# Layer 0 of a four-layer model: attention scores by single heads in two row tiles, and low parts, cosines and unpacking rearranged

## What is computed

```python
q, k, v = (proj(wq), proj(wk), proj(wv))          # 32 heads of 16
q = _apply_rope(q, sin, cos)                       # x*cos + rot*sin
k = _apply_rope(k, sin, cos)
scores = jnp.einsum('bnth,bnsh->bnts', q, k) * (1.0 / math.sqrt(h))
scores = jnp.where(causal, scores, -jnp.inf)
attn = jax.nn.softmax(scores, axis=-1)
out = jnp.einsum('bnts,bnsh->bnth', attn, v)       # then @ wo.T

Wg, Wu, Wd = _dequant(gate...), _dequant(up...), _dequant(down...)   # (w4 - (z4 + 1)) * s
h = jax.nn.silu(xf @ Wg) * (xf @ Wu)
out = h @ Wd
```

## Time and profile before

| | us |
|---|---|
| median of 3 runs | 2555.86 (2555.06 to 2556.41) |
| the profiled execution | 2561.34 |
| its span | 2559.6 |
| busy: PE / PE weight loads | 2455.2 (96%) / 1962.8 (77%) |
| busy: DVE / ACT / POOL | 1618.1 (63%) / 1102.4 (43%) / 618.3 (24%) |
| attention of layer 0, first score to first wo matmul | 337.6 to 480.4 |

### The profile page before, as it was taken

One profiled execution on the slowest core, in us unless ns is written; L12 is line 12 of the kernel. 1 busy time (PEld: TensorE's weight loads), 2 busy tenths in 40 slices (PEclk: granted clock), 3 DMA queues, 4 the chain that ended last, 5 costly groups with the idle time before them and its releaser, 6 DMA issues. The chain is left out here.

```text
span 2559.6 us, 40914 instructions
## 1 busy us (share of the span) xinstructions
PE 2455.2 (96%) x14448; PEld 1962.8 (77%) x14448; DVE 1618.1 (63%) x2388; ACT 1102.4 (43%) x2158; POOL 618.3 (24%) x455
## 2 busy tenths in 40 slices
PE   5989999999989989999999999999999999999899
PEld 4767777778866668888888878888888877888666
DVE  5886567864477776545444467777777776543576
ACT  3322145443255533223333366666666653323453
POOL 3343110246321226124444400000000024430100
PEclk8999999999989999999999999999999999999999
DMA  2232164122332212234444332222222222322421
GB/s 86 62 101 83 52 122 88 31 38 43 57 89 59 48 28 42 45 98 140 148 148 143 125 114 87 83 90 90 68 75 86 66 44 39 53 46 33 102 63 37
DMA packets 406207, 195.33 MB, mean 76 GB/s; under 512 B 280393, under 2 KB 359729, under 8 KB 406079
## 3 DMA queue, kind: packets, MB, share of 16 engines
q1 hardware_dynamic: 404860, 191.53, 30.0%
q10 hardware_dynamic: 1218, 2.06, 0.3%
HBM read 129.85 MB, written 44.04 MB: 68 GB/s over the span
## 5 line engine op out<-in xcount | busy, mean ns | idle before, releaser
L603 PE MATMUL banks<-xn_hi,w_hi 128*128 128x512 f32 x1264 | 496.6, 393 | 12.9 <-ACT sgf L1146 10.0
L603 PE MATMUL banks<-xn_lo,w_hi 128*128 128x512 f32 x1264 | 493.1, 390 | 0.0
L603 PE MATMUL banks<-xn_hi,w_lo 128*128 128x512 f32 x1264 | 492.9, 390 | 0.0
L603 PEld LDWEIGHTS banks<-xn_hi,w_hi 128*128 128x128 f32 x1264 | 238.0, 188 | 64.4 <-DVE w_lo L591 10.4
L603 PEld LDWEIGHTS banks<-xn_hi,w_lo 128*128 128x128 f32 x1264 | 237.9, 188 | 49.7
L603 PEld LDWEIGHTS banks<-xn_lo,w_hi 128*128 128x128 f32 x1264 | 238.1, 188 | 48.4
L591 DVE TENSOR_TENSOR w_lo<-tw,w_hi 128x512 fp32r<-128x512 f32 (+2 forms) x136 | 117.0, 867 | 201.8 <-ACT w_hi L583 201.7
L2719 DVE TENSOR_SCALAR raw<-banks,cols 128x512 f32<-128x512 f32 x128 | 103.7, 810 | 180.3 <-ACT sq L2702 180.3
L2731 POOL TENSOR_TENSOR ssq<-ssq,sq 128x512 f32<-128x512 f32 x128 | 165.1, 1290 | 183.2 <-ACT sq L2702 183.2
L469 POOL TENSOR_TENSOR nat<-nat,wscale 128x512 f32<-128x512 f32 (+1 forms) x44 | 51.5, 1179 | 651.6 <-DMA nat<-in_L_ffn_w 651.4
L1258 POOL TENSOR_TENSOR h_lo<-sgf,h_hi 128x512 fp32r<-128x512 f32 (+1 forms) x94 | 128.1, 1367 | 288.8 <-ACT h_hi L1149 288.8
(11 more groups left out here) (302 smaller groups left out, 5831.5 us busy)
## 6 DMA issues: line engine op xcount, KB each, us to landing
qk_scratch<-raw SPq DMA_DIRECT2D x64, 512.0 KB, 3.0
qk_raw<-qk_scratch SPq DMA_DIRECT2D x64, 512.0 KB, 3.8
nat<-in_L_ffn_w SPq DMA_DIRECT2D x48, 256.0 KB
head_scratch<-stage SPq DMA_DIRECT2D x16, 512.0 KB, 3.2
st_qs<-st_hi SPq DMA_DIRECT2D x128, 64.0 KB, 2.1
nat<-in_L_attn_Wq SPq DMA_DIRECT2D x32, 256.0 KB
nat<-in_L_attn_Wk SPq DMA_DIRECT2D x32, 256.0 KB
nat<-in_L_attn_Wv SPq DMA_DIRECT2D x32, 256.0 KB
```

The costliest lines, as they stand in the source:

```text
L603: mm = nc.tensor.matmul(to[half][:, :], w[0:n, j, k * P:(k + 1) * P], r, start=first and k == 0 and x == 0, stop=last and k == len(rows) - ...
```

## The change

1. **Attention of layer 0.** New functions `pe_att0`, `dve_att0`, `act_att0`, `sp_att0` take the place of the common ones there. Single heads have 48 rows (three terms of 16); one head of each pair lies in rows 0 to 63, the other (e = 1) in rows 64 to 127, so that a matmul of 48 (or 52, with four rows of tops) contracts in one half of the rows. `both` issues a score step in one half and a shift step in the other, alternating matmul by matmul, and waits at its head for what both need. Masks are two bf16 matmuls per step in 64 rows (`square`, `row64`). PE's order per chunk: three double steps, values (first key block, e = 0), tops, two double steps, values (the other three groups), one double step. ACT copies the tops to `neg_tops`, and SP brings them into the query rows by two DMAs per chunk; a chunk's first double step waits for these (`tops_in`).
2. **Loads.** A unit has twelve DMAs of 128 KB. The first three units wait for `shift_rows`, the end of six casts of 32x2048 on DVE (before, three of 32x4096); POOL's memsets of the keys are gone, and it makes two small casts. Later units are split into keys and queries, each behind the tops of one chunk.
3. **Low parts of xn** in all layers, and the **cosine products** of q and k in layer 0, are made by DVE alone; POOL keeps its share of the rotated pieces' low parts.
4. **Unpacking** is a function of its own, done for the next chunk between multiply and low part. The first down chunk is spread, unpacked, dequantized and given its high part in the last gate/up round.

```diff
-        def dve_dequant(dve, s, i, j, parts):
+        def dve_unpack(dve, s, i, j, parts):
 
             dve.wait_ge(loaded[j].sem, loaded_count(s, i, j))
             for n, (r, c) in enumerate(parts):
                 v = nat[r, j, c].bitcast(I32)
                 ins = nc.vector.tensor_scalar(v, v, shift[r, 0:1], 15, ALU.logical_shift_right, ALU.bitwise_and)
             ins.then_inc(unpacked.sem, 1)
+
+        def dve_dequant(dve, s, i, j, parts):
+
             dve.wait_ge(unpacked.sem, s.un0 + i + 1)
             dve.wait_ge(turned.sem, s.turned0 + i + 1)
             dve.wait_ge(lo.sem, s.lo0 + before(i, 2))
...
             ins.then_inc(dequant.sem, 1)
+            if i + 1 < s.n:
+                dve_unpack(dve, s, i + 1, (i + 1) % SLOTS, parts_of(s, i + 1))
+            dve_lo(dve, s, i, j, parts)
...
         def dve_low_x(dve, s, half):
-            for k in range(0, KT, 2):
-                low_x(dve, nc.vector, s, half, k)
-
-        def pool_low_x(pool, s, half):
-            for k in range(1, KT, 2):
-                low_x(pool, nc.gpsimd, s, half, k)
+            for k in range(KT):
+                low_x(dve, s, half, k)
...
+            def down_ahead(left):
+                if left == 1:
+                    dve_unpack(dve, s.then, 0, 0, parts_of(s.then, 0))
+                    dve_dequant(dve, s.then, 0, 0, parts_of(s.then, 0))
+
+            up_rounds(dve, s, ahead, work, opening, LEAD if s.tw is None else LEAD_TURN, first, pair, 1,
+                      down_ahead if s.then else seam_dve(dve, s))
...
+            if opening and s.up and s.up.then is s:
+                load(0, 0, s.chunks[0])
...
+                nc.vector.tensor_tensor(seqs(v), seqs(v), bcast(cst[:, C_COS0:C_COS0 + SEQ], 2), ALU.mult).then_inc(step_c.sem, 1)
                 nc.vector.tensor_tensor(seqs(rot), seqs(rot), bcast(cst[:, C_SIN0:C_SIN0 + SEQ], 2), ALU.mult)\
...
-        def pool_piece(pool, s, n):
-
-            tile, half = PIECES[n]
-            pool.wait_ge(step_a.sem, s.a0 + n + 1)
-            v = seqs(heads0.tiles[tile][2][:, at(half)])
-            nc.gpsimd.tensor_tensor(v, v, bcast(cst[:, C_COS0:C_COS0 + SEQ], 2), ALU.mult).then_inc(step_c.sem, 1)
...
-            rows = slice(ROWS, P)
             dve.wait_ge(used.sem, s.used0)
-            for stacks in unit_ks:
-                ins = nc.vector.tensor_copy(stacks[rows, :, :, :].rearrange("p j e t -> p (j e) t"),
-                                            tail_bcast(cst[rows, C_NEG:C_NEG + HPC], HALF))
+            for e in range(2):
+                rows = slice(e * ROW_TILE + QUAD, (e + 1) * ROW_TILE)
+                for stacks in unit_ks:
+                    ins = nc.vector.tensor_copy(stacks[rows, :, :], tail_bcast(cst[rows, C_NEG1:C_NEG1 + PAIRS], HALF))
             ins.then_inc(shift_rows.sem, 1)
 
         def pool_v0(pool, s):
             pool.wait_ge(used.sem, s.used0)
-            for stacks in unit_ks:
-                nc.gpsimd.memset(stacks[0:ROWS, :, :, :].bitcast(F32), 0.0).then_inc(slot_clear.sem, 1)
+            pool.wait_ge(square_in.sem, square_in.count)
+            nc.gpsimd.tensor_copy(square[:, :, :, :].rearrange("p a b n -> p (a b n)"), square_f[:, 0:4 * P])
+            nc.gpsimd.tensor_copy(row64[:, :], square_f[:, 4 * P:]).then_inc(square_ready.sem, 1)
...
+        def unit_load(sp, s, u, kind, e):
+            half, c = divmod(u, QC)
+            slot = u % UNIT_SLOTS
+            src = head_dram["kq".index(kind), c, :, :, :, at(half)].rearrange("j r x t -> r j x t")[e * HD:(e + 1) * HD]
+            for x, part in enumerate((0, 0, 1) if kind == "k" else (0, 1, 0)):
+                rows = slice(e * ROW_TILE + x * HD, e * ROW_TILE + (x + 1) * HD)
+                sp.dma_start((unit_ks if kind == "k" else unit_qs)[slot][rows, :, :].bitcast(F32), src[:, :, part, :])\
+                  .then_inc(unit_in[slot].sem, 16)
+
+        def sp_units(sp, s):
+
+            for j in range(SLOTS):
+                sp.wait_ge(stage_out[j].sem, in0.st0[j] + 16 * len(PIECES) // SLOTS)
+            sp.wait_ge(shift_rows.sem, s.neg + 1)
+            for u in range(UNIT_SLOTS):
+                for kind in "kq":
                     for e in range(2):
-                        rows = slice(x * ST + e * HD, x * ST + (e + 1) * HD)
-                        sp.dma_start(ks[rows, :, e, :].bitcast(F32), k[e * HD:(e + 1) * HD, :, part, :])\
-                          .then_inc(unit_in[slot].sem, 16)
+                        unit_load(sp, s, u, kind, e)
+
+        def sp_tops(sp, s, i):
+
+            chunk, seq, slot = att_place(s, i)
+            sp.wait_ge(top_copied.sem, s.tc + i + 1)
+            for e in range(2):
+                row = e * ROW_TILE + TERMS
+                sp.dma_start(unit_qs[slot][row:row + PAIRS, :, i % 2 * SEQ:(i % 2 + 1) * SEQ].bitcast(F32),
+                             bcast(neg_tops[e * PAIRS:(e + 1) * PAIRS, i % 2, :].bitcast(F32), PAIRS)).then_inc(tops_in[i % 2].sem, 16)
+
+        def sp_att0(sp, s, chunks):
+
+            for i in chunks:
+                sp_tops(sp, s, i)
+                u = (i + 3) // 2
+                if UNIT_SLOTS <= u < UNITS:
+                    if i % 2:
+                        sp.wait_ge(shifted.sem, s.sh + 2 * STEPS * (u - UNIT_SLOTS + 1))
+                        for e in range(2):
+                            unit_load(sp, s, u, "k", e)
+                    else:
+                        u = (i + 2) // 2
+                        for e in range(2):
+                            unit_load(sp, s, u, "q", e)
...
+        def score_heads(part):
+
+            return (0, part, 0, PAIRS) if part < 2 else (1, part % 2, 2 * (part // 2 - 1), 2)
+
+        def shift_heads(part):
+
+            return (0, part % 2, 2 * (part // 2), 2) if part < PAIRS else (1, part % 2, 0, PAIRS)
+
+        def pe_att0(pe, s):
...
+                if there:
+                    kb, e2, p2_, n_p2 = shift_heads(part2)
+                    m = STEPS * j + part2
+                    if m >= 2:
+                        pe.wait_ge(exp_done.sem, s.ex + m - 1)
+                    if part2 == 0:
+                        pe.wait_ge(tops_in[j % 2].sem, s.ti[j % 2] + 32 * (j // 2 + 1))
...
+                for b in range(2):
+                    if here:
+                        nc.tensor.matmul(o[:, :, qt * P + b * ROW_TILE:qt * P + (b + 1) * ROW_TILE], square[tile(e, ROW_TILE), 0, b, :],
+                                         bcast(row64[tile(e, ROW_TILE), :], n_p), start=b == 0, stop=False, skip_group_check=True)
+                    if there:
+                        nc.tensor.matmul(o2[:, :, b * ROW_TILE:(b + 1) * ROW_TILE], square[tile(e2, ROW_TILE), 1, b, :],
+                                         bcast(row64[tile(e2, ROW_TILE), :], n_p2), start=b == 0, stop=False, skip_group_check=True)
+                for x in range(PAIRS):
+                    if here and x < n_p:
+                        mm = nc.tensor.matmul(o[:, x, :], q[tile(e, TERMS), p + x, qt * P:(qt + 1) * P], k[tile(e, TERMS), p + x, 0:keys],
+                                              start=False, stop=x == n_p - 1, skip_group_check=True)
+                        if x == n_p - 1:
+                            mm.then_inc(s_ready.sem, 1)
+                    if there and x < n_p2:
+                        mm = nc.tensor.matmul(o2[:, x, :], k2[tile(e2, TERMS + PAIRS), p2_ + x, kb * P:(kb + 1) * P],
+                                              q2[tile(e2, TERMS + PAIRS), p2_ + x, kb * P:SEQ],
+                                              start=False, stop=x == n_p2 - 1, skip_group_check=True)
+                        if x == n_p2 - 1:
+                            mm.then_inc(shifted.sem, 1)
...
+            for i in range(-3, CHUNKS):
+                for n in range(3):
+                    both(i + 2, 3 + n, i + 1, n)
+                values(i, 0, 0)
+                tops(i + 2)
+                for n in range(2):
+                    both(i + 3, n, i + 1, 3 + n)
+                values(i, 0, 1)
+                values(i, 1, 0)
+                values(i, 1, 1)
+                both(i + 3, 2, i + 1, 5)
...
+            def copy_tops(i):
+                if not inside(i):
+                    return
+                act.wait_ge(top_turned.sem, s.tt + i + 1)
+                nc.scalar.activation(neg_tops[0:HPC, i % 2, :], bank[5][0:HPC, i % 2 * SEQ:(i % 2 + 1) * SEQ], ACT.Copy)\
+                  .then_inc(top_copied.sem, 1)
...
+        up0.then = down0
...
-            sp_units(sp, att0, range(UNIT_SLOTS))
+            sp_units(sp, att0)
             sp_proj(sp, wo0, True)
             sp_proj(sp, wo0)
-            sp_units(sp, att0, range(UNIT_SLOTS, UNITS))
+            sp_att0(sp, att0, [0])
             sp.wait_ge(cleared.sem, 4)
             adapter_load(sp, adapters[0])
+            sp_att0(sp, att0, [1])
             adapter_load(sp, adapters[1])
+            sp_att0(sp, att0, [2])
             sp_columns(sp)
```

(1 more changed line is left out.)

240 lines of the change are left out of this document (188 added, 52 removed).

## The result

The changed kernel takes 2615.97 us (median of 4 runs, 2615.51 to 2618.96) against 2556.14 before: the ratio is 1.0237, with a 95% interval of 1.0219 to 1.0254. It is 60 us slower, outside the range of 2534 to 2574. The profiled run's span grew from 2559.6 to 2613.7 us, 54.1 more; it is less than 60 because the profiled execution of the kernel before was itself some 5 us above the median.

The account below looks back on a forecast made before the run. The prediction took TensorE's own instructions to set the pace in attention, and its waits elsewhere. Its terms summed to +1.0 on the profiled 2561.3 us, 2562.3, less 5.5 to the median: 2556.8, range 2534 to 2574.

Parts of the forecast that it names:

- Gate/up: Layer 0's gate/up stage: shorter DVE rounds cut PE's waits for the gated product, -6.3 us (bounds -3 to -12.6).
- seam: Gate/up to down stage: preparing the first down chunk early removes waits for dequantized columns, -5.0 us (-3.5 to -5.7).
- Low parts of xn: Making them on DVE alone mostly removes PE's waits for them, -3.0 us (bounds 0 to -3.6).
- Start: Attention's first shift waits for tops queued on SP behind unit and wo loads, +25.5 us (bounds +18 to +30).
- half clock behind the stall: After the stall at attention's start PE runs at half clock for a while, +1.5 us (bounds 0 to 3).
- Fourth chunk: Attention: its tops stand on SP behind 19 bias and column loads, +6 us (bounds +4 to +8).
- Period: Steady attention: time per chunk falls from 8.73 to 7.4 us, -20.7 us in all (bounds -27 to -10).
- rule on draining: Attention: switching tile mode drains PE; three more changes per chunk at 0.2 us, +9.4 us where PE is the bound.
- B: Rival, attention: the two tiles' weight loads run one after another, period 8.0 to 8.1, total 2566 us; chance 0.15.
- C: Rival, attention: the two tiles don't run at once at all, period 8.7, total 2577 us; chance 0.08.
- D: Rival, attention's start: at most half as late as forecast, total 2530 to 2543 us; chance 0.2.
- Uncovered: Attention: adapters' and wo's turns no longer fit DVE's free time and delay a reduction, +3 us (+1 to +6).

Follow-up runs that it names:

- parts_no_low: Kernel before plus the change's parts outside attention, but odd low parts of xn stay on POOL: 2549.40 us against 2556.53, ratio 0.9967.
- wo_late: Changed kernel with wo's four loads issued one or two at a time behind the tops of chunks 0 to 2, not ahead of the first: 2596.3 us.
- act_tops: Changed kernel with each chunk's tops DMAs issued from ScalarE's queue and SP's order as in the kernel before: 2589.33 us, ratio 1.0139.
- no_later_loads: Changed kernel without the loads of units 3 to 7, all else kept: 2582.3 us.
- loads_free: Changed kernel without loads of units 3 to 7, columns before units, first tops behind two units, adapters and wo behind later tops: 2553.3 us, ratio 0.9986.
- before_q16: Kernel before with each query load of 32 rows split into two of 16: 2563.2 us against 2556.0.

## Why the prediction was wrong, step by step

**Gate/up, -6.3 and seam, -5.0.** The mechanism held, the size was little more than half. The first score came 6.7 us earlier, not 11.3. In the changed kernel the cosine and sine products take what was forecast:

```profile
129.40 0.68 DVE L1959 TENSOR_TENSOR at_x<-at_x,cst 128x512 f32<-128x512 f32 x1
129.99 0.69 DVE L1960 TENSOR_TENSOR rot<-rot,cst 128x512 f32<-128x512 f32 x1
```

Of the longer two waits 1.80 and 2.19 us are left (forecast 1.5 and 3.0), of the four short ones 3.1 (forecast nothing; 3.0 before, so they did not shrink at all). The seam is the mis-sized term: 0.21 and 2.89 us remain of 3.8. The first chunk came ahead, the second is dequantized after the gated product as before, and PE still stands for it. I counted the wait as gone and did not ask what is late next.

**Low parts of xn, -3.0.** Nothing came: 3.5 us of waits after, 3.6 before, and parts_no_low is not slower. Four in a row on DVE are no earlier than two beside two; the waits became fewer and longer.

**Start, +25.5; it was +36.3.** The order on SP, the mechanism, was right. Two terms were mis-sized, in opposite directions, by 13.3 us for the data and 4.2 for the casts. The rate of the units' data was taken from loads of 32 and 16 rows mixed (211), and all of them have 16 rows after the change: 35.7 us in place of 22.4. The casts, which I had at 12 us, made up for a part of it:

```profile
307.68 7.82 DVE L2102 CAST ks<-cst 32x2048 fp32r<-32x2048 f32 x6
```

Six in 7.82 us, 1.3 each, without POOL's memsets, where I halved the 3.98 of one of 32x4096 and had 2 each. SP's issue of wo took 33.3, not 24.9. wo's share of the wait, 22 us by wo_late, is near the 19.4 of the sum. The half clock behind the stall, +1.5 with bounds of 0 to 3, was too small as well: the clock is at 0.50 for some 13 us after the first shift, with PE busy for 12 of them, which is some 6 us lost.

**Fourth chunk, +6.** 5.45 us of wait, as forecast, though in part by luck: SP issued the columns in 11.3 us (388.56 to 399.88), not 13.9, and the chunk beside them was no period of 7.4 but one of 13.3.

**Period, -20.7; the step that failed.** The loop itself was right: 7.16 without loads, tiles at once. The step that failed is that only PE's and DVE's instructions bound the period, with no term for transfers; measured were 161.4 us from the first shift to wo (136.2 before), and not 20.7 less. A unit's loads and the tops' transfers must share the DMA engines within the period. A unit brings 1.57 MB in two chunks: at 132 GB/s 11.9 of 14.3 us. The change gives the queries of a unit one period's notice, and they missed it by up to 2.9 us; where loads go out earlier, the tops miss theirs by 4 to 5 (act_tops). The one shown above is followed by some 7 us at half clock. I had looked at DMA only for the start; the rows gave the bytes, and the sum could have been made for the period as well. The half clock, counted for one stall, came back with every second chunk.

**The rule on draining.** The changes of shape were in the loop at 0.2 us each, and the loop came out at 7.16 against 7.4 forecast. These runs give no reason for a higher price.

**The rivals.** B and C (tiles not at once) did not come. A score head and a shift head start 0.02 us apart:

```profile
446.84 0.36 PE L2380 MATMUL banks<-ks,qs 48*128 48x256 f32 x1
446.86 0.36 PE L2385 MATMUL banks<-qs,ks 52*128 52x256 f32 x1
```

Close starts alone don't prove it, since the ends of matmuls are modelled. The length of double steps does; two of them in no_later_loads, and the values behind them:

```profile
414.96 0.21 PE L2366 MATMUL banks<-row,square 64*128 64x128 bf16 x1 [0.36 <-ACT p_front L2789]
...
415.45 0.21 PE L2366 MATMUL banks<-row,square 64*128 64x128 bf16 x1
...
415.95 0.41 PE L2410 MATMUL banks<-at_p,at_rows 128*32 128x256 f32 x2
```

Each takes 0.49 to 0.50 us. It holds 1024 columns of heads and 512 of masks, which one after another would be 0.64 us at 2.4 GHz, so the two tiles do overlap; B needed 0.8. My own 0.65 to 0.7 was too long for these too.

D was the opposite of what happened. The outcome was a case that had no name in the prediction; the rival that ends on the slow side was looked for in TensorE and not in the transfers.

**Uncovered, +3.** With nothing else late (loads_free) the adapters' two chunks cost 7.7 us over two periods of 7.16, half clock again among them (0.60 and 0.54 from 440 to 448); my bound was 6. In the kernel before the same transposes cost next to nothing: its two chunks took 9.22 and 9.02 us against 8.73.

**The version that beats both.** The kernel before with unpacking ahead, the cosines on DVE and the first down chunk ahead: 2549.4, 0.33% faster than before (0.9967, 0.9955 to 0.9979). The attention in two tiles has no part in it.

**What stays open.** How the loss of the steady part splits between standing and half clock was not measured apart: no run held the clock up through the waits. An estimate from rows: in no_later_loads PE is busy 37.84 of 40 us at full clock, so 15.6 periods of 7.16 would be 111.7 us, 105.7 of them busy; in the changed kernel it is busy 135.0 of 162 us (373 to 535). That is 21 us more of standing and 29 more for the same matmuls, so by this estimate the half clock cost at least as much as the waits. Nor was it tried to bring the new row layout in by loads of 32 rows that land in the right places; that would need another layout in DRAM.

## What to carry to other kernels

When a stage gets faster, make the sum of bytes per period at the rate of the new transfer shape, not only the engines' sums: here 83% of the shorter period was load data, and two transfers of 16 KB that every chunk needs had to pass through it. A step that goes through DMA in every iteration replaces a wait of under 1 us by one that depends on all other traffic. Where PE waits 2 to 3 us in each round, count the half-clock stretch behind it as well: 7 us at half clock are, by these numbers, 3.5 us of work lost beside a wait of 2.9.

## What the runs showed of the hardware

- Loads from DRAM in 2 KB pieces, 128 KB each onto 16 rows (partitions), ran at 126 to 138 GB/s; 256 KB each onto 32 rows at 217; a stream with half of its bytes in either kind at 205. The DMA engines' share was full (0.99 to 1.07) in all of them.
- Two 16 KB transfers from another engine's queue, issued at 337.3 while some 1.9 MB of SP's load data were still to come (an estimate: 14.4 us at 132 GB/s), let PE go at 351.7, 14 us later and together with the end of that data (act_tops). The profile shows no landing of its own for them.
- Four loads of 256 KB in 128-byte pieces held SP's queue for 24.9 to 35.3 us when issued in a row behind other loads (before, before_q16), and 0.6 us each when issued singly (wo_late, loads_free). In wo_late one such issue, at 338.68 with unit data still in flight, took 0.56, and the three adapter loads behind it held the queue for 15.97.
- Six casts of 32x2048 took DVE 7.82 us without memsets on POOL; three of 32x4096 with POOL's memsets beside them took 14.14.
- PE kept its full clock with a pause of 0.36 us in every 7.16 (no_later_loads, 420 to 460), and was granted half for about 7 us after a pause of 2.9 (after, 438 to 445).
